# A gated cross-attention block: the next group's q, k and raw scores one body ahead, and norms from summed squares

## The chip, the cores and the metric

The kernel runs on one core of a Trainium2 chip. The metric is device time in microseconds (us). The kernel before takes 1311.98 us, the median of three runs (1311.91 to 1312.0). The engines are PE (TensorE), ACT (ScalarE), DVE (VectorE), POOL (GpSimd) and SP, which here only issues DMAs.

## The reference

The input x has 64 batches of 64 tokens with 256 features, and the context has the same shape. Four residual sub-blocks follow each other; the change touches the first.

```
def rms_norm(x, scale, eps=1e-6):
    ms = mean(square(x), axis=-1, keepdims=True)      # over all 16*128 = 2048 features
    return x * rsqrt(ms + eps) * scale
# 1. cross attention, 16 heads of 128
q   = rms_norm(layernorm(x) @ q_w + q_b, nq_s)        # split into heads after the norm
k   = rms_norm(ctx @ ki_w + ki_b, nki_s)
v   = ctx @ vi_w + vi_b
out = softmax(q k^T / sqrt(128)) v                    # in each batch and head, 64 x 64 scores
x   = x + tanh(g_xattn[0]) * (out @ o_w + o_b)
# 2. a dense layer plus the two best of 8 low-rank experts   3. a sigmoid attention on the raw context
# 4. the best of 8 larger experts; each with a layernorm before it and a tanh gate behind it
```

(The context is shorter than the reference's 257 image tokens, so the text branch is empty and only the image weights enter.)

## The kernel before

**Tiling.** The 4096 tokens are 8 groups of 512 (four tiles of 128 tokens, or 8 batches). Every engine runs its own program with the same skeleton: one body for each group b, and in it 16 steps, one for each head h. Products in float32 precision are made from a rounded high part and a remainder (`_hi`, `_lo`), three matmuls for each product (`three`, L113).

**One step** on PE is: scores of the last two heads (even steps only), `project` of k for head h (six matmuls of 512 columns), `attend` for head h-3, `values` for h, `project` of q for h, `prob_transpose` for h-2, `output` for h-3. The points "a" to "e" between them take side work (`share`): N is the next group's preparation (layernorm, transposes, norms), S the later sub-blocks of group b-1, T the last sub-block of group b-2. ACT copies every product out of its bank (`project`), takes the exponentials (`exps`) and rounds the attention output (`attn_hi`). DVE makes `logits`, `probabilities`, `attn_lo` and half of each copy `prob_copy`. Nothing but this written order and the semaphores sets the sequence. The products k, v, q use two banks in turn, and the scores of a pair of heads one bank, from which `logits` reads them directly.

**The norms.** The sum of squares of a token's 2048 q features is obtained without q: with the Gram matrix G = W W^T made once at the start (`turn_weight`, `gram_matrix`, 64 transposes and 128 matmuls), it is x G x^T plus terms in the bias. `gram_products` (L983) makes x G for each tile of x and context, `gram_sums` (L1503) multiplies with x and sums. `square_norms` and `norm_factors` take the reciprocal root on 8 columns, `norms` (L995) spreads the k factors over all rows with a matmul of ones and a diagonal, and `score_factors` (L1531) makes the 64 x 64 factors `rr` of each tile, by which `logits` multiplies.

**Weights.** The q and k weights stay in SBUF, as `w_hi` and `w_lo`. The v and output weights come from DRAM scratch in pairs of heads, 512 KB each, into two buffers.

```
        def step(b, h):                       # PE, L1255, cut
            if h % 2 == 0 and live(b, h - 2):
                scores(b, h - 2)
                scores(b, h - 1)
            project(b, h, 0)                  # k
            attend(b, h - ATT_LAG)            # ATT_LAG = 3
            values(b, h)
            project(b, h, 2)                  # q
            prob_transpose(b, h - TURN_LAG)   # TURN_LAG = 2
            output(b, h - OUT_LAG)            # OUT_LAG = 3
```

## Time and profile before

| | us |
|---|---|
| median of 3 runs | 1311.98 |
| the profiled execution | 1310.84 |
| its span | 1309.0 |
| PE busy | 1294.2 |
| DVE busy | 765.1 |
| ACT busy | 727.3 |
| POOL busy | 67.7 |

The span runs from the first to the last instruction of the profiled execution; 1.84 us of that run lie around it. The granted clock of TensorE was 1.00, which is 2.4 GHz, in all 40 slices of the span. Busy times are unions: matmuls are pipelined, so a matmul's printed duration is longer than the distance to the next one, and costs on PE are read as distances between starts.

### The profile page before, as it was taken

What the parts mean: (1) busy time and instruction counts of PE and PEld (TensorE: products, weight loads), DVE (VectorE), ACT (ScalarE), POOL (GpSimd) and SP (SyncE); (2) the same over time, 40 slices, a digit from 0 to 9 for tenths busy, and PEclk for the clock granted to TensorE, in tenths of its full rate; (3) what the DMA queues carried; (4) which work ended last, traced back from release to release, by engine and by line L of the source; (5) the groups of instructions that cost most, each with busy time, mean ns of one, the idle gap of its engine ahead of it and who ended that gap; (6) DMA issues with size and microseconds to landing.
All of it is one profiled execution on the core that took longest, in us unless ns stands there. A gap on an engine that the chain in (4) does not pass through costs nothing.

```text
span 1309.0 us, 26268 instructions
## 1 busy us (share of the span) xinstructions
PE 1294.2 (99%) x10249; PEld 1143.4 (87%) x10249; DVE 765.1 (58%) x2309; ACT 727.3 (56%) x2037; POOL 67.7 (5%) x112
## 2 busy tenths in 40 slices
PE   8999999999999999999999999999999999999998
PEld 8889889988998889988899888998889988898887
DVE  7645656646565565655556465564656646564585
ACT  4365756556465564655545655546646556556522
POOL 0000000000000000010000100001000000001010
PEclk9999999999999999999999999999999999999999
DMA  8221441132222231223212232123312112212101
GB/s 323 105 97 49 150 142 65 46 101 97 66 65 81 77 102 66 65 66 129 74 41 81 66 113 81 49 66 98 111 51 82 49 66 97 66 51 78 50 1 49
DMA packets 42985, 108.44 MB, mean 83 GB/s; under 512 B 3696, under 2 KB 22384, under 8 KB 42096
## 3 DMA queue, kind: packets, MB, share of 16 engines
q1 hardware_dynamic: 42864, 106.77, 24.1%
q8 instruction: 83, 1.36, 0.4%
q14 instruction: 38, 0.31, 0.1%
HBM read 94.17 MB, written 12.58 MB: 82 GB/s over the span
## 4 chain that ended last, share of the span: by engine, by line
PE 92%; DVE 4%; ACT 2%; issue 1%; DMA 1%; SPq 0%; DVEq 0%; ACTq 0%
PE bank L116 63%; PE bank L1022 8%; PE bank L1032 5%; PE bank L991 3%; PE bank L1132 2%; PE bank L1144 2%; PE bank L1011 2%; PE bank L1086 1%; PE bank L970 1%; PE bank L1176 1%; ACT logit L734 1%; DMA raw<-in_L_xattn_q_w_dram 1%; PE bank L998 0%; PE bank L1153 0%; DVE wt L1461 0%
## 5 line engine op out<-in xcount | busy, mean ns | idle before, releaser
L734 ACT ACTIVATE logit<-logit,least 128x64 f32<-128x64 f32 x512 | 171.1, 337 | 180.5 <-DVE least L1569 180.5
L116 PE MATMUL bank<-sv,ct_hi 128*128 128x256 f32 x1024 | 195.8, 290 | 0.0
L116 PE MATMUL bank<-so,ao_hi 128*128 128x256 f32 x1008 | 193.8, 291 | 0.1
L116 PEld LDWEIGHTS bank<-sv,ct_hi 128*128 128x128 f32 x1024 | 158.2, 188 | 13.1 <-issue 10.7
L116 PEld LDWEIGHTS bank<-so,ao_hi 128*128 128x128 f32 x1008 | 153.4, 188 | 7.8 <-issue 7.6
L1022 PEld LDWEIGHTS bank<-pt,v_sb 128*128 128x128 f32 x1024 | 133.7, 191 | 11.3 <-ACT pt L742 0.3
L116 PE MATMUL bank<-sv,ct_lo 128*128 128x256 f32 x512 | 142.8, 279 | 0.0
L752 ACT ACTIVATE v_sb<-bank 128x512 f32<-128x512 f32 x128 | 76.1, 594 | 119.6 <-PE bank L116 119.6
L116 PE MATMUL bank<-so,ao_lo 128*128 128x256 f32 x504 | 140.5, 279 | 0.0
L1557 DVE SCALAR_TENSOR_TENSOR ao_lo<-bank,vecs,ao_hi 128x512 fp32r<-128x512 f32 x126 | 94.6, 751 | 76.7 <-ACT ao_hi L728 76.5
L1022 PE MATMUL bank<-pt,v_sb 128*128 128x128 f32 x1024 | 134.8, 274 | 0.1
L755 ACT ACTIVATE q_sb<-bank,qbias,qscale 128x512 f32<-128x512 f32 x128 | 98.6, 770 | 50.6 <-PE bank L116 50.6
L1551 DVE COPY pt<-bank 64x256 f32<-64x256 f32 x128 | 54.8, 428 | 97.3 <-PE bank L1011 95.6
L116 PE MATMUL bank<-ct_hi,k_hi 128*128 128x512 f32 x256 | 109.1, 426 | 0.7 <-DVE ct_lo L1544 0.7
L116 PE MATMUL bank<-xt_hi,q_hi 128*128 128x512 f32 x256 | 104.2, 407 | 1.7 <-ACT k_sb L748 1.6
L748 ACT ACTIVATE k_sb<-bank,vecs 128x512 f32<-128x512 f32 x128 | 86.1, 673 | 29.4 <-PE bank L116 29.3
L116 PE MATMUL bank<-ct_lo,k_hi 128*128 128x512 f32 x256 | 101.1, 395 | 0.0
L116 PE MATMUL bank<-xt_lo,q_hi 128*128 128x512 f32 x256 | 101.1, 395 | 0.0
L116 PE MATMUL bank<-xt_hi,q_lo 128*128 128x512 f32 x256 | 101.0, 395 | 0.0
L116 PE MATMUL bank<-ct_hi,k_lo 128*128 128x512 f32 x256 | 101.0, 394 | 0.0
L734 ACT ACTIVATION_READ_ACCUMULATOR logit<-logit,least 128x1 f32 x512 | 97.0, 189 | 0.0
L116 PEld LDWEIGHTS bank<-sv,ct_lo 128*128 128x128 f32 x512 | 96.2, 188 | 0.0
(235 smaller groups left out, 2518.4 us busy)
## 6 DMA issues: line engine op xcount, KB each, us to landing
sv<-v_scratch SPq DMA_DIRECT2D x56, 512.0 KB, 3.4
so<-o_scratch SPq DMA_DIRECT2D x56, 512.0 KB, 3.3
xin<-in_x_dram SPq DMA_DIRECT2D x8, 512.0 KB, 4.5
cin<-in_ctx_pairs_dram SPq DMA_DIRECT2D x8, 512.0 KB, 5.8
cs<-in_ctx_turned_dram SPq DMA_DIRECT2D x8, 512.0 KB, 4.6
xres<-in_x_dram SPq DMA_DIRECT2D x8, 512.0 KB, 4.8
v_scratch<-sv SPq DMA_DIRECT2D x8, 512.0 KB, 2.8
o_scratch<-so SPq DMA_DIRECT2D x8, 512.0 KB, 2.8
```

The source lines that it names most:

```text
L116: last = pe.matmul(out, lhs[a], rhs[b], start=start and n == 0, stop=stop and n == 2, **kw)
L734: last = act.activation(logit[:, h % 2, t, :], logit[:, h % 2, t, :], ACT.Exp, scale=-1.0, bias=least[:, h % 2, t:t + 1], accum_out=rsum[: ...
L748: act.activation(k_sb[:, h % 2, :], bank[:, :], ACT.Identity, bias=vecs[:, 3 * H + h:3 * H + h + 1]).then_inc(pj_read.sem, 1)
L752: act.activation(v_sb[:, (h // 2) % 2, t:t + 2, :], bank[:, :].rearrange("p (t n) -> p t n", t=2), ACT.Copy).then_inc(pj_read.sem, 1)
L755: act.activation(q_sb[:, h % 2, :], bank[:, :], ACT.Identity, scale=qscale[:, h:h + 1], bias=qbias[:, h:h + 1]).then_inc(pj_read.sem, 1)
L991: last = pe.matmul(dst[:, c * P:D + 1], src[:, c, t * P:(t + 1) * P], gram[:, n, c, c * P:D + 1], start=c == 0, stop=c == DC - 1)
L1011: last = pe.transpose(bank[:, q * P:(q + 1) * P], prob[:, 2 * q:2 * q + 2, :].rearrange("p t l -> p (t l)"), ident[:, :])
L1022: last = pe.matmul(dst[:, q, i], v_sb[:, (h // 2) % 2, 2 * q + i, (h % 2) * HD:(h % 2 + 1) * HD], pt[:, q, i, :], start=True, stop=True)
L1032: last = pe.matmul(at_ps[i * SEQ:(i + 1) * SEQ, (h % 2 * NT + t) * SEQ:(h % 2 * NT + t + 1) * SEQ], q_sb[:, h % 2, s], k_sb[:, h % 2, keys ...
L1132: last = pe.matmul(dst[i][:, c * D:(c + 1) * D], xn[rows, t, c * P:(c + 1) * P], cin2[rows, t, :], start=True, stop=True)
L1551: dve.tensor_copy(pt_part(1), turned_probs(g, h, 1)).then_inc(pt_ready[1].sem, 1)
L1557: dve.scalar_tensor_tensor(out=lo[:, :], in0=attention_bank(g, h)[:, :], scalar=vecs[:, v:v + 1], in1=hi[:, :].bitcast(F32), op0=ALU.add, ...
```

## The change

There is one more body, b = -1. In body b the engines now make k, q and the scores of group b+1, while v, the softmax, the attention and the output are those of group b. The raw scores are copied by DVE into `raw_score` in SBUF (`score_copy`, one copy for two heads), and `logits` reads them there a body later. The last body makes no k, q or scores. Two context buffers alternate. The layernorm and transposes of a group come two bodies ahead.

The Gram matrices and products are gone. ACT squares q out of the bank (`project_q`); POOL squares k and adds both up over the heads (`add_squares`); in step 0 of group b's own body `norms` sums over partitions with a matmul of ones (k, as a row) and four one-column matmuls (q). DVE then takes the reciprocal root on 260 columns in step 1 (`score_factors`).

The q and k weights are split in body -1, written to DRAM scratch, and from group 1 on fetched in pairs of heads, 1 MB each, into two buffers (`fetch_weights`).

```diff
+        def add_squares(g, h):                                   # POOL, each head of each group
+            total = k_sum[:, g % 2, :], q_sum[:, g % 2, :]
+            pool.wait_ge(k_read.sem, k_read.count(g, h))
...
+            pool.tensor_tensor(k_sq[:, h % 2, :] if h else total[0], k_sb[:, h % 2, :], k_sb[:, h % 2, :],
+                               ALU.mult).then_inc(k_squared.sem, 1)
+            if h:
...
+                pool.tensor_tensor(total[0], total[0], k_sq[:, h % 2, :], ALU.add).then_inc(k_added.sem, 1)
+                pool.wait_ge(q_squared.sem, q_squared.count(g, h))
...
+                pool.tensor_tensor(total[1], total[1], q_sq[:, h % 2, :], ALU.add).then_inc(q_added.sem, 1)
...
+        def project_k(g, h):                                     # ACT
+            act.wait_ge(k_full.sem, k_full.count(g, h))
+            k_squared.wait(act, g, h - 2)
...
+        def project_q(g, h):                                     # ACT
+            act.wait_ge(q_full.sem, q_full.count(g, h))
...
+            if h:
+                q_added.wait(act, g, -1 if h == 1 else h - 3)
+            act.activation(q_sq[:, h % 2, :] if h else q_sum[:, g % 2, :], bank[:, :], ACT.Square,
+                           bias=vecs[:, h:h + 1]).then_inc(q_squared.sem, 1)
...
-        def gram_products(b, t):                                 # PE
...
-        def norms(b):
-            dst = take("rk", 0, b + 1)
-            pe.wait_ge(diag_ready.sem, diag_ready.count(b + 1, 0))
-            pe.matmul(dst[:, :], ones[:, :], diag[:, :, :].rearrange("p t n -> p (t n)"),
-                      start=True, stop=True).then_inc(rk_full.sem, 1)
+        def norms(g):
+            row, column = take("rk", 0, g), take("rq", 0, g)
+            pe.wait_ge(k_added.sem, k_added.count(g, H - 2))
+            pe.matmul(row[:, :], ones[:, :], k_sum[:, g % 2, :], start=True, stop=True)
+            pe.wait_ge(q_added.sem, q_added.count(g, H - 2))
+            for t in range(NT):
+                last = pe.matmul(column[:, t:t + 1], q_sum[:, g % 2, t * P:(t + 1) * P], ones[:, 0:1],
+                                 start=True, stop=True)
+            last.then_inc(rk_full.sem, 1)
...
         def step(b, h):                                          # PE
-            main = live(b, h)
...
+            main = live(b + 1, h)
+            if h % 2 == 0 and live(b + 1, h - 2):
+                scores(b + 1, h - 2)
+                scores(b + 1, h - 1)
+            if main and (b >= 0 or h >= FIRST_K):
+                project("k", b + 1, h)
             share(b, h, "a")
             if live(b, h - ATT_LAG):
                 attend(b, h - ATT_LAG)
             share(b, h, "b")
-            if main:
+            if live(b, h):
                 values(b, h)
             share(b, h, "c")
...
             if main:
+                project("q", b + 1, h)
...
-        def gram_sums(g, t):                                     # DVE
...
+        def score_factors(g):
...
+            rsqrt_guess(dve, chain, rqk[:, :], nqk_t[:, :], squares[:, :])
+            rsqrt_newton(dve, chain, rqk[:, :], nqk_t[:, :], squares[:, :], 3)
+            for t in range(NT):
+                last = dve.tensor_scalar(rr[:, g % 2, t, :], rqk[:, t * SEQ:(t + 1) * SEQ],
+                                         rqk[:, NT * SEQ + t:NT * SEQ + t + 1], -float(HD) ** -0.5, ALU.mult, ALU.mult)
             last.then_inc(rr_ready.sem, 1)
 
+        def score_copy(g, h):
+            dve.wait_ge(scores_full.sem, scores_full.count(g, h // 2))
+            at = h % H
+            dve.tensor_copy(raw_score[:, at:at + 2, :, :].rearrange("p h t l -> p (h t l)"),
+                            at_ps[:, :]).then_inc(scores_read.sem, 1)
...
-            chain.link(dve.tensor_tensor(logit[:, u, :, :], at_ps[:, u * NT * SEQ:(u + 1) * NT * SEQ].rearrange(
-                "p (t l) -> p t l", t=NT), rr[:, (g - (h < 0)) % 2, :, :], ALU.mult))
+            chain.link(dve.tensor_tensor(logit[:, u, :, :], raw_score[:, h % H, :, :], rr[:, (g - (h < 0)) % 2, :, :],
+                                         ALU.mult))
...
+            if "F" in parts:
+                if at == (0, "c"):
+                    mean_squares(b)
+                if at == (1, "b"):
+                    score_factors(b)
```

**PE at the start.** Before, in the order of the program (`raw` and `wt` are the q weights and their transpose); the same again for k follows the last row:

```order
L1294 MATMUL bank<-ident,ones 128x128 x3
L962 MATMUL bank<-ident,raw 128x128 x24
L970 MATMUL bank<-wt 128x257 x4
L970 MATMUL bank<-wt 128x129 x4
L962 MATMUL bank<-ident,raw 128x128 x4
L970 MATMUL bank<-wt 128x257 x4
```

Now (`wqk` is the buffer of q and k weights):

```order
L1349 MATMUL bank<-ident,ones 128x128 x24
L116 MATMUL bank<-ct_hi,wqk 128x512
L116 MATMUL bank<-ct_lo,wqk 128x512
L116 MATMUL bank<-ct_hi,wqk 128x512 x2
L116 MATMUL bank<-ct_lo,wqk 128x512
```

The first k product stands directly behind 24 matmuls that only keep PE at work; the transposes and Gram matrices are gone.

**POOL.** Before, all that it does up to the second group's work:

```order
L640 MEMSET pt 128x512
L646 TENSOR_TENSOR xres<-xres,obias 128x256 [waits xres_in,s_obias]
L646 TENSOR_TENSOR xres<-xres,obias 128x256 x3
L654 TENSOR_TENSOR xres<-xres,bias 128x256 [waits xn1_ready]
L654 TENSOR_TENSOR xres<-xres,bias 128x256 x3
```

Now, at the same place; the last three rows repeat for each head of each group:

```order
L696 MEMSET pt 128x512
L703 TENSOR_TENSOR k_sum<-k_sb 128x512 [waits k_read]
L703 TENSOR_TENSOR k_sq<-k_sb 128x512 [waits k_read]
L709 TENSOR_TENSOR k_sum<-k_sum,k_sq 128x512 [waits k_squared]
L713 TENSOR_TENSOR q_sum<-q_sum,q_sq 128x512 [waits q_squared]
L703 TENSOR_TENSOR k_sq<-k_sb 128x512 [waits k_read]
L709 TENSOR_TENSOR k_sum<-k_sum,k_sq 128x512 [waits k_added,k_squared]
L713 TENSOR_TENSOR q_sum<-q_sum,q_sq 128x512 [waits q_added,q_squared]
```

POOL has gained three operations of 512 columns for each head, and ACT waits for two of them.

**DVE in step 1 of a body** (here body 1; `pt` is the transposed probabilities, `squares` the mean squares). Before:

```order
L1557 SCALAR_TENSOR_TENSOR ao_lo<-bank5,vecs,ao_hi 128x512
L1551 COPY pt<-bank5 64x4x64
L1567 TENSOR_TENSOR logit<-bank4,rr 128x256
L1569 TENSOR_REDUCE least<-logit 128x4
L1567 TENSOR_TENSOR logit<-bank4,rr 128x256
```

Now; two more rounds of the last three rows and the four factors `rr` follow, and only then the copy `pt` and the logits:

```order
L1551 SCALAR_TENSOR_TENSOR ao_lo<-bank5,vecs,ao_hi 128x512
L74 TENSOR_SCALAR nqk_t<-squares 128x260
L75 TENSOR_SCALAR rqk<-nqk_t 128x260
L80 TENSOR_TENSOR nqk_t<-rqk 128x260
L81 SCALAR_TENSOR_TENSOR nqk_t<-nqk_t,squares 128x260
L82 SCALAR_TENSOR_TENSOR rqk<-nqk_t,rqk 128x260
```

A chain of eleven operations on 260 columns has moved in ahead of the copy that PE's `attend` waits for.

## Rows read from the trace of the kernel before

**Rows 1.** Busy time, share of the span and instructions of each engine.
```profile
PE 1294.2 (99%) x10249; PEld 1143.4 (87%) x10249; DVE 765.1 (58%) x2309; ACT 727.3 (56%) x2037; POOL 67.7 (5%) x112
```
**Rows 2.** Windows: stretch, length, busy us by engine, clock, DMA share, GB/s.
```profile
622.00:778.80 156.80, 156.69 (x1253) 138.60 (x1252) 90.97 (x282) 88.39 (x254) 8.32 (x12) 1.00 0.24 78
1091.00:1227.00 136.00, 135.90 (x1082) 119.39 (x1082) 73.36 (x208) 77.71 (x227) 8.32 (x12) 1.00 0.18 59
1238.00:1309.00 71.00, 63.48 (x453) 53.75 (x451) 48.70 (x151) 20.85 (x45) 5.11 (x8) 1.00 0.07 23
```
**Rows 3.** Timeline: start, us, engine, line, operation, count [idle before]; POOL.
```profile
682.02 3.01 POOL L654 TENSOR_TENSOR xres<-xres,bias 128x256 f32<-128x256 f32 x4 [95.79 <-ACT xn L761]
...
838.86 3.00 POOL L654 TENSOR_TENSOR xres<-xres,bias 128x256 f32<-128x256 f32 x4 [96.44 <-ACT xn L761]
```
**Rows 4.** Timeline of PE at the start and at one even step.
```profile
38.09 0.48 PE L116 MATMUL bank<-ct_hi,k_hi 128*128 128x512 f32 x1
...
39.57 0.82 PE L991 MATMUL bank<-gram,xs 128*128 128x257 f32 x4
...
44.74 0.48 PE L116 MATMUL bank<-sv,ct_hi 128*128 128x256 f32 x2
...
47.63 0.40 PE L116 MATMUL bank<-ct_hi,k_hi 128*128 128x512 f32 x1
...
49.03 0.40 PE L116 MATMUL bank<-sv,ct_hi 128*128 128x256 f32 x2
...
50.43 1.02 PE L998 MATMUL bank<-diag,ones 128*128 128x512 f32 x2
...
636.32 1.15 PE L1032 MATMUL bank<-k_sb,q_sb 128*64 128x64 f32 x32
```
**Rows 5.** Timeline of DVE and ACT at the start.
```profile
4.65 0.17 DVE L1902 TENSOR_TENSOR bsq<-vecs 128x16 f32<-128x16 f32 x1 [4.65 <-DMA vecs<-in_columns_dram]
...
11.40 1.40 DVE L1491 BATCH_NORM_STATS2 stats<-xin 128x6 f32<-128x256 f32 x4
...
14.92 0.37 DVE L87 BATCH_NORM_AGGREGATE moment<-stats 128x2 f32<-128x6 f32 x4
...
17.71 0.16 DVE L1500 SCALAR_TENSOR_TENSOR shift<-moment,rstd 128x4 f32<-128x4 f32 x1
...
17.91 2.08 ACT L708 ACTIVATE xin<-xin,shift,rstd 128x256 f32<-128x256 f32 x4
```
**Rows 6.** Groups by form on POOL: busy us, mean ns, idle before.
```profile
L654 POOL TENSOR_TENSOR xres<-xres,bias 128x256 f32<-128x256 f32 x32 | 23.8, 780 | 781.7 <-ACT xn L761 781.7
...
L664 POOL TENSOR_TENSOR x<-x,csum 128x256 f32<-128x256 f32 x24 | 15.0, 657 | 270.9 <-ACT xn L761 270.9
```
**Rows 7.** One line's durations: minimum/median/maximum ns.
```profile
L654 POOL TENSOR_TENSOR xres<-xres,bias x32: 724/737/938, 211.6 to 1256.2; 128x256 f32<-128x256 f32 x32
```
**Rows 8.** Groups by form on DVE and ACT.
```profile
L1461 DVE COPY wt<-bank 128x512 f32<-128x512 f32 x16 | 10.2, 685 | 3.9 <-PE bank L962 3.9
...
L1567 DVE TENSOR_TENSOR logit<-bank,rr 128x256 f32<-128x256 f32 x128 | 53.7, 420 | 56.2 <-PE bank L1032 54.8
...
L755 ACT ACTIVATE q_sb<-bank,qbias,qscale 128x512 f32<-128x512 f32 x128 | 98.6, 770 | 50.6 <-PE bank L116 50.6
```
**Rows 9.** Timeline of DVE in steps 0 to 2 and in step 6.
```profile
630.07 0.42 DVE L1576 TENSOR_TENSOR prob<-logit,rinv 128x256 f32<-128x256 f32 x1
...
634.47 0.43 DVE L1551 COPY pt<-bank 64x256 f32<-64x256 f32 x1 [2.48 <-PE bank L1011]
...
637.52 0.42 DVE L1567 TENSOR_TENSOR logit<-bank,rr 128x256 f32<-128x256 f32 x1 [1.02 <-PE bank L1032]
...
641.17 0.75 DVE L1557 SCALAR_TENSOR_TENSOR ao_lo<-bank,vecs,ao_hi 128x512 fp32r<-128x512 f32 x1 [0.63 <-ACT ao_hi L728]
...
683.51 0.92 DVE L1576 TENSOR_TENSOR prob<-logit,rinv 128x256 f32<-128x256 f32 x1
```
**Rows 10.** DMA issues: KB each, median us from issue to landing.
```profile
sv<-v_scratch SPq DMA_DIRECT2D x56, 512.0 KB, 3.4
```

More of the change, by code:

```diff
@@ L1051, in output, with bank_for @@
             last.then_inc(o_full.sem, 1)
-        def bank_for(g, u):
-            pj_read.wait(pe, g, u - 2)
-            return pj_ps[u % 2]
+        def bank_for(kind, g, h):
+            bank, before = PRODUCT[kind, g, h]
+            if before is not None:
+                kind_before, group, head = before
+                pe.wait_ge(READ[kind_before].sem, READ[kind_before].count(group, head))
+            return bank
         def values(g, h):
-            b, p = bank_for(g, 3 * h + 1), h // 2
+            b, p = bank_for("v", g, h), h // 2
+            ct_hi, ct_lo = context[g % 2]
             if is_body(g, 0):
@@ L1514, in square_norms @@
-        def square_norms(g):
-            dve.wait_ge(gr_read.sem, gr_read.count(g, 2 * NT - 1))
-            for n in range(2):
-                half = slice(n * NT, (n + 1) * NT)
-                chain.mark(dve.tensor_scalar(sums_b[:, half], sums[:, half], beta[:, n:n + 1],
-                                             1.0 / INNER, ALU.add, ALU.mult))
-            chain.wait()
-            chain.link(dve.tensor_scalar(sums_b[:, :], sums_b[:, :], RMS_EPS, None, ALU.add))
-            rsqrt_guess(dve, chain, rqk[:, :], nqk_t[:, :], sums_b[:, :])
-            rsqrt_newton(dve, chain, rqk[:, :], nqk_t[:, :], sums_b[:, :], 1)
@@ L1825, in step @@
                 logits(b, h - 1)
-            if main and h == 0 and not is_body(b, 0):
-                split(b, 1)
+            if h == 0 and 0 <= b < NG - 1:
+                split(b + 1, 1)
             if h % 2:
```

627 lines of the change are left out of this document (277 added, 350 removed).

## The prediction, made before the changed kernel ran

> **What bounds the kernel now.** I read the page's busy times first: PE is busy for 99% of the span, DVE for 58%, ACT for 56% and POOL for 5% [rows 1]. The windows say the same of one full body, PE 156.7 of 156.8 us [rows 2], and the bodies repeat at 838.86 - 682.02 = 156.8 us [rows 3]. TensorE's clock was granted at 1.00 (2.4 GHz) throughout. So before is a queue of PE work with hardly a gap: what leaves PE shortens the time one for one, as long as no other engine gets in its way. Only the tail from 1238 us on has waits, 7.5 us in 71 [rows 2], and the change leaves that alone. The questions are how much PE work goes, what the new first body costs, and whether DVE and POOL can still keep ahead.
>
> **PE work.** Costs are distances between starts. One k product is 49.03 - 47.63 = 1.40 us, one v product 50.43 - 49.03 = 1.40, the scores of two heads 1.15, the Gram products of one group 44.74 - 39.57 = 5.17 [rows 4]. The old `norms` matmul is at most its 1.02 us; I take 0.9. The new one adds four one-column products, which the trace does not show. From below a score matmul gives 1.15/32 = 0.036 us for each of eight passes, 0.3 us; from above, the old norms matmul once more, 0.9. I take 0.9, nearer to a full weight load, so new norms cost 1.8. A steady body then has 156.8 - 5.2 - 0.9 + 1.8 = 152.5 us of PE work.
>
> **The count.** I compare the two kernels at one point: in before, PE at 44.74 us, with k(0,0) and the Gram products of group 0 done; in after, PE as it leaves `norms` of group 0 in body 0. From 44.74 to the end of before are 1309.0 - 44.7 = 1264.3 us. Of these the new kernel has by then done, or never does:
> - 16 q and 16 more k products: 32 x 1.40 = 44.8
> - v(0,0): 1.4, and 16 heads of scores: 8 x 1.15 = 9.2
> - seven groups of Gram products: 7 x 5.17 = 36.2
> - eight old norms for seven new: 8 x 0.9 - 7 x 1.8 = -5.4
>
> Sum 86.2, so 1178.1 us of PE work remain behind that point.
>
> **When is that point?** The start: before, PE worked 38 us until the first k product [rows 4], on transposes and Gram matrices. These go, and what is late next is the input. Vectors landed at 4.65; the tokens, second in the old queue and now first, I put at 7. Behind them stand the statistics, 1.4, and variance and scale, 17.71 + 0.16 - 14.92 = 3.0, to 11.4. Then the normalising, 2.1 [rows 5], the rounding of q's first weights, the wait for k(0,1), the transposes' copies and the split of x; about 8.5 us by ACT and DVE operations of 0.6 to 1.2 each. So q(0,0) starts at 20 (17 to 25).
>
> In body -1 PE needs 2 x 1.40 + 0.58 = 3.4 us for each head. ACT needs less than 3. POOL does three operations of 512 columns. The trace has POOL only at 256 columns: 0.737 us with two full inputs, 0.612 to 0.657 where one is broadcast, 0.938 at worst [rows 6, 7]. Twice that bounds 512 columns between 1.22 (less if part is fixed cost) and 1.88; I take 1.4, just under twice 0.737, since both inputs are full. Three make 4.2, with the waits on itself 4.3 us a head. That is longer than PE's 3.4, and ACT waits for it: k of head h for the squares of h-2, q for the sum of h-3. So body -1 runs at POOL's pace. The first two heads' sums end at about 25; fourteen more take 60, to 85.4, and the norms end at 86.4. If PE set the pace it would be 75, with 1.88 us an operation 106.
>
> The Trainium skill ("GPSIMD Engine Reference", § 3.1) has 4497 ns for a POOL `tensor_tensor` add of 2048 columns; as an estimate that is 1.12 us for 512, 3.5 a head, and body -1 would be at PE's pace. This trace's 0.737 for 256 is above that rate, but part of it may be fixed. The sum would be 11 us less by the page.
>
> Without any new waits the span is 86.4 + 1178.1 = 1264.5 us.
>
> **DVE and POOL in the full bodies.** DVE had 91.0 us of work in 156.8 [rows 2]. It loses the Gram sums and gains eight copies of scores at 0.69 [rows 8] = 5.5, and eleven root steps on 260 columns at about 0.46 (0.42 for 256 columns [rows 8] and the link) = 5.1; net +3 us. The sum is hidden, but its place is not. In step 1 the chain and `rr`, some 6 us, stand ahead of the copy `pt`. Before, DVE sat idle for 2.48 us in front of that copy at 634.47, and 1.02 in front of the logits [rows 9]. So about 3.5 us are covered, `attend`, logits and `attn_lo` behind them are late by 2 to 3, and PE gets some of it. The logits no longer wait for scores, which gives part back. I take 1 us a body.
>
> POOL, idle before, is now at work for 16 x 4.3 + 8.3 = 77 us of a body. The trace shows what that does: `prob`, two SBUF inputs, takes 0.42 us, and 0.92 at 683.51, while POOL's bias additions run (682.02 to 685.03); one POOL operation in that line took 0.938 instead of 0.737 [rows 3, 7, 9]. Each waits for the other. The logits, which read a bank and `rr`, now read `raw_score` and `rr` and join this kind. With POOL at work half the time and 32 large and some 60 small such operations, I put +15 us on DVE: 109 of 152.5. That is covered on average, not where DVE was dense. I take 1 us a body of PE wait; nothing and 6 are the bounds. Together 2 x 7 = 14 us.
>
> This is the place of the Trainium skill's rule ("SBUF — State Buffer", § Who interferes with whom): a DVE instruction with two SBUF inputs contends with a GpSimd instruction that reads SBUF, and the loser blocks for the other's whole instruction. The row's 0.5 us against an operation of 0.74 agrees in kind. By full blocking the second rival below comes nearer.
>
> **The last body** has no k, q or scores: 136.0 - 44.8 - 8 = 83 us of PE. DVE keeps 73.4 - 1.2 = 72 [rows 2], 87%, in a chain exponentials - `prob` - transpose - `pt` - `attend` - `ao_hi` - `ao_lo` - `output` in which 2.8 us of cover a step are gone. I take 9 us of waiting, between 0 and 25.
>
> **ACT** gains one square a head (nearest row the q copy, 0.77 [rows 8]), 12 us on 88.4 of 152.5: hidden. **The weights:** 1 MB each two steps; 512 KB land in 3.4 us [rows 10], so about 7 against two steps of 9.5: hidden. In body -1 the writes of pair 2 queue behind 6 MB of loads and could hold ACT for a few us, where POOL is the bound anyway: nothing.
>
> **Sum.** 1264.5 + 14 + 9 = 1287.5 of span, +1.8 around it = 1289.3; the median shown stands 1.1 above the profiled run's 1310.84. Forecast **1290 us**.
>
> **Rivals.**
> 1. *Everything is covered.* POOL needs 3.6 us a head (-10), no waits in full bodies (-14), 4 in the last (-5): 1261 us. For it: in a full body PE waits for 0.1 us only [rows 2]. Against it: the row at 683.51 [rows 9].
> 2. *DVE becomes the bound in bodies 0 to 6 (slower).* The place is DVE beside POOL's 48 additions a body. DVE has 94 us of its own; if nearly each of POOL's 60 operations blocks it for 0.9 us or more, it reaches 94 + 54 = 148, and with its dependences PE waits for it. Each us over a body's 152.5 counts seven times; before's time is reached when a body waits 5.5 us rather than 2. At 8 us: 1290 + 7 x 6 = 1332. For it: the blocking is in the trace; against it: only half of each POOL operation blocked there.
> 3. *Body -1 is long.* POOL at 1.8 us an operation, or late weights: +15 to +20, 1308 us. For it: DVE's splitting of weights reads SBUF twice as well.
> 4. *The clock.* All rows show 1.00, the tail with 11% of waits too [rows 2]. In body -1 PE would be at work for 3.4 of 4.3 us. At 1.2 GHz a head takes 6.8, 16 x 2.5 = 40 us more: 1330. The Trainium skill ("TensorE: Matmul & The Clock Gate", Part 1) has the throttled state as the default that activity releases. No row here shows a fall.
>
> **Chances.** Forecast (1273 to 1305) 0.50; rival 1 0.20; rival 2 0.14; rival 3 0.12; rival 4 0.04. The range, from rival 1 to short of rival 2, is 1258 to 1325. A measurement tells 0.2%, 2.6 us, from no change. Slower takes most of rivals 2 and 4: 0.15; same 0.04; faster 0.81.
>
> **What would show it.** Right: the first k product at 13 us instead of 38; POOL without gaps in body -1 and `norms` of group 0 at about 86; bodies of 154 to 155 us by POOL's bias additions; `prob` and `logit` above 0.42 us in the mean; PE waits at `pt`, `attend` and `output` in step 2. Wrong: PE waits in every step (rival 2), a granted clock below 1.00 (4), or `norms` of group 0 before 78 or after 98 us.

## The result, and the profile after

The changed kernel takes 1423.8 us (median of 4 runs, 1418.5 to 1426.2) against 1312.0 (4 runs) for the kernel before on the same chip. The ratio is 1.085, 95% interval [1.083, 1.086]: slower by 112 us, where I had forecast 22 us faster. The range ended at 1325. The profiled execution took 1418.5 us, its span 1416.7; it is the fastest of the four, so differences of medians and of spans can disagree by some 5 us.

The page's busy line, as [rows 1]:

```profile
PE 1283.8 (91%) x9889; PEld 1114.4 (79%) x9889; DVE 878.7 (62%) x2164; ACT 802.1 (57%) x2177; POOL 522.2 (37%) x480
```

PE is busy for 10 us less than before, but the span is 108 us longer: PE waits for 133 us. DVE has 114 us more busy time. The windows, as [rows 2] (stretch, length, busy us of PE, PEld, DVE, ACT, POOL, clock, DMA share, GB/s): one full body, the last body, the tail.

```profile
611.73:782.56 170.83, 157.36 (x1228) 137.33 (x1228) 106.10 (x265) 97.31 (x269) 64.83 (x58) 0.98 0.35 118
1222.24:1345.70 123.46, 102.87 (x720) 91.23 (x720) 80.44 (x234) 63.14 (x219) 8.27 (x12) 0.93 0.22 73
1345.00:1416.70 71.70, 62.48 (x450) 53.28 (x448) 48.66 (x151) 20.41 (x43) 5.12 (x8) 1.00 0.07 23
```

The tail is what it was. A full body is 14 us longer, and PE is idle for 13.5 us of it. The periods come from POOL's bias additions, as in [rows 3]:

```profile
611.73 2.98 POOL L726 TENSOR_TENSOR xres<-xres,bias 128x256 f32<-128x256 f32 x4 [3.20 <-ACT xn L851]
...
782.56 2.98 POOL L726 TENSOR_TENSOR xres<-xres,bias 128x256 f32<-128x256 f32 x4 [3.20 <-ACT xn L851]
```

The start and both ends of the account, from PE's timeline (start, us, line, operands [idle before]): the first k product, q(0,0), and `norms` of groups 0 and 7, each with its one-column products (L1051) as its end.

```profile
12.62 0.76 PE L116 MATMUL bank<-ct_hi,wqk 128*128 128x512 f32 x1 [3.76 <-DVE wqk L1480]
...
22.45 0.77 PE L116 MATMUL bank<-xt_hi,wqk 128*128 128x512 f32 x1 [3.19 <-issue]
...
97.17 1.02 PE L1048 MATMUL bank<-k_sum,ones 128*128 128x512 f32 x2
98.12 1.05 PE L1051 MATMUL bank<-ones,q_sum 128*128 128x1 f32 x8
...
1222.24 1.10 PE L1048 MATMUL bank<-k_sum,ones 128*128 128x512 f32 x2 [0.94 <-issue]
1223.17 0.95 PE L1051 MATMUL bank<-ones,q_sum 128*128 128x1 f32 x8
```

Cut at the points where PE leaves `norms`, forecast and trace compare so:

```
                                  forecast   trace   difference
start to norms of group 0             86.4    99.2      +12.8
bodies 0 to 6                       1030.6  1124.9      +94.3
last body and tail                   170.5   192.6      +22.1
span                                1287.5  1416.7     +129.2
```

The forecast of the last row but one is the time of before behind v(7,0), from 1094.98 us, less 31 products of q and k and 16 heads of scores, plus 9 us of waiting: 1309.0 - 1095.0 - 43.4 - 9.2 + 9 = 170.5. It can't be taken from the recorded 83 us, since the window for it ended at 1227 [rows 2], and the last step of before's body was still to come:

```profile
1232.38 0.48 PE L116 MATMUL bank<-xt_hi,q_hi 128*128 128x512 f32 x1
```

**What a wait looks like.** Step 6 of a full body has PE's longest. DVE from 442.25 us, and POOL beside it:

```profile
442.25 0.88 DVE L1570 TENSOR_TENSOR prob<-logit,rinv 128x256 f32<-128x256 f32 x1
443.19 0.75 DVE L1551 SCALAR_TENSOR_TENSOR ao_lo<-bank,vecs,ao_hi 128x512 fp32r<-128x512 f32 x1
443.86 0.90 DVE L80 TENSOR_TENSOR nt_t<-rstd 128x4 f32<-128x4 f32 x1
444.79 0.16 DVE L81 SCALAR_TENSOR_TENSOR nt_t<-nt_t,var_eps 128x4 f32<-128x4 f32 x1
444.98 1.15 DVE L82 SCALAR_TENSOR_TENSOR rstd<-nt_t,rstd 128x4 f32<-128x4 f32 x1
446.17 0.16 DVE L80 TENSOR_TENSOR nt_t<-rstd 128x4 f32<-128x4 f32 x1
446.36 1.15 DVE L81 SCALAR_TENSOR_TENSOR nt_t<-nt_t,var_eps 128x4 f32<-128x4 f32 x1
...
449.01 0.68 DVE L1601 TENSOR_TENSOR x2t_lo<-bank,x2t_hi 128x512 fp32r<-128x512 f32 x1
```
```profile
443.70 1.04 POOL L703 TENSOR_TENSOR k_sq<-k_sb 128x512 f32<-128x512 f32 x1
444.81 1.30 POOL L709 TENSOR_TENSOR k_sum<-k_sum,k_sq 128x512 f32<-128x512 f32 x1
446.24 1.26 POOL L713 TENSOR_TENSOR q_sum<-q_sum,q_sq 128x512 f32<-128x512 f32 x1
```

Three operations on four columns, 0.16 us each by themselves, start while a POOL operation runs and end at most 0.02 us behind it: at 444.76, 446.13 and 447.51, where POOL ends at 444.74, 446.11 and 447.50. So DVE waits out the rest of POOL's instruction. Larger operations wait in the same way, but end later. In a `logit` of this kernel, POOL ends at 672.38, and DVE, which needs 0.42 by itself, at 672.66, 0.28 us behind:

```profile
671.09 1.29 POOL L713 TENSOR_TENSOR q_sum<-q_sum,q_sq 128x512 f32<-128x512 f32 x1 [0.94 <-ACT q_sq L845]
671.13 1.53 DVE L1561 TENSOR_TENSOR logit<-raw_score,rr 128x256 f32<-128x256 f32 x1
```

Back in step 6, `ao_lo`, with a bank and one SBUF tile as its two large inputs, takes its usual 0.75 [rows 9] in the same stretch. `x2t_lo` is late by 3 us, and PE waits:

```profile
449.84 0.66 PE L116 MATMUL bank<-late_w_hi,x2t_hi 128*128 128x392 f32 x1 [3.47 <-DVE x2t_lo L1601]
450.30 0.53 PE L116 MATMUL bank<-late_w_lo,x2t_hi 128*128 128x392 f32 x1
```
```profile
446.00:448.00 2.00, 0.37 (x4) 0.16 (x2) 1.83 (x6) 0.64 (x2) 1.37 (x2) 1.00 0.34 68
448.00:450.00 2.00, 0.16 (x1) 0.19 (x2) 1.90 (x6) 0.00 (x0) 0.00 (x0) 0.66 0.50 195
450.00:452.00 2.00, 2.00 (x7) 2.00 (x8) 1.97 (x3) 0.00 (x0) 0.00 (x0) 0.50 0.00 0
...
454.00:456.00 2.00, 2.00 (x11) 1.83 (x10) 0.19 (x2) 2.00 (x10) 0.00 (x0) 0.63 0.00 0
```

The granted clock (the number behind POOL's) falls from 1.00 to 0.50 (2.4 to 1.2 GHz) near the end of that idle stretch, and PE works on at half speed until about 455. Such a fall stands in each of bodies 0 to 5, and the last body, where PE waits most, has a mean of 0.93.

Over the run, the DVE forms with two SBUF inputs got longer, those with one did not (compare [rows 8, 9]):

```profile
L1561 DVE TENSOR_TENSOR logit<-raw_score,rr 128x256 f32<-128x256 f32 x128 | 76.0, 593 | 0.8
L1532 DVE COPY raw_score<-bank 128x512 f32<-128x512 f32 x64 | 43.6, 682 | 0.4
L82 DVE SCALAR_TENSOR_TENSOR rstd<-ntmp,rstd 128x4 f32<-128x4 f32 x72 | 24.6, 342 | 2.5
```

### The profile page after: what moved, and what is told of

It reads as the page before. It is cut to its first block, busy times and chain, and to the rows that moved or that the text cites. A ratio compares the mean times of both kernels' runs of the same rounds, so it can differ in the third digit from the quotient of the medians.

```text
span 1416.7 us, 26442 instructions
## 1 busy us (share of the span) xinstructions
PE 1283.8 (91%) x9889; PEld 1114.4 (79%) x9889; DVE 878.7 (62%) x2164; ACT 802.1 (57%) x2177; POOL 522.2 (37%) x480
## 3 DMA queue, kind: packets, MB, share of 16 engines
q8 instruction: 81, 1.33, 0.4%
## 4 chain that ended last, share of the span: by engine, by line
PE 54%; DVE 26%; ACT 12%; issue 5%; POOL 3%; DMA 0%; SPq 0%; POOLq 0%; ACTq 0%; DVEq 0%
PE bank L116 38%; PE bank L1076 5%; ACT logit L815 4%; ACT xn L851 2%; DVE rstd L82 2%; PE bank L1197 2%; PE bank L1209 2%; DVE ao_lo L1551 2%; PE bank L1087 2%; DVE stats L1586 2%; ACT k_sb L828 2%; PE bank L1065 1%; DVE ntmp L81 1%; ACT ao_hi L809 1%; POOL k_sum L709 1%
## 5 line engine op out<-in xcount | busy, mean ns | idle before, releaser
L703 POOL TENSOR_TENSOR k_sq<-k_sb 128x512 f32<-128x512 f32 x120 | 129.4, 1079 | 369.1 <-ACT k_sb L828 369.1
L713 POOL TENSOR_TENSOR q_sum<-q_sum,q_sq 128x512 f32<-128x512 f32 x120 | 160.0, 1333 | 263.3 <-ACT q_sq L845 262.5
L116 PE MATMUL bank<-xt_hi,wqk 128*128 128x512 f32 x512 | 190.2, 413 | 27.4 <-ACT k_sb L828 22.7
L116 PE MATMUL bank<-ct_hi,wqk 128*128 128x512 f32 x512 | 194.8, 422 | 10.1 <-ACT k_sb L828 4.5
L116 PE MATMUL bank<-so,ao_hi 128*128 128x256 f32 x1008 | 199.7, 296 | 1.5 <-DVE ao_lo L1551 1.3
L116 PEld LDWEIGHTS bank<-so,ao_hi 128*128 128x128 f32 x1008 | 158.4, 194 | 10.4 <-issue 10.0
L709 POOL TENSOR_TENSOR k_sum<-k_sum,k_sq 128x512 f32<-128x512 f32 x120 | 156.0, 1300 | 9.4
L116 PEld LDWEIGHTS bank<-xt_hi,wqk 128*128 128x128 f32 x512 | 98.8, 193 | 52.9 <-ACT k_sb L828 27.2
L116 PEld LDWEIGHTS bank<-ct_hi,wqk 128*128 128x128 f32 x512 | 100.3, 196 | 33.7 <-ACT k_sb L828 4.9
L1569 DVE RECIPROCAL rinv<-rsum 128x4 f32<-128x4 f32 x128 | 22.5, 176 | 143.7 <-ACT logit L815 143.5
L828 ACT ACTIVATE k_sb<-bank,vecs 128x512 f32<-128x512 f32 x128 | 86.4, 675 | 35.6 <-PE bank L116 35.4
```

The lines of the kernel that those rows point to most:

```text
L116: last = pe.matmul(out, lhs[a], rhs[b], start=start and n == 0, stop=stop and n == 2, **kw)
L703: pool.tensor_tensor(k_sq[:, h % 2, :] if h else total[0], k_sb[:, h % 2, :], k_sb[:, h % 2, :], ALU.mult).then_inc(k_squared.sem, 1)
L709: pool.tensor_tensor(total[0], total[0], k_sq[:, h % 2, :], ALU.add).then_inc(k_added.sem, 1)
L713: pool.tensor_tensor(total[1], total[1], q_sq[:, h % 2, :], ALU.add).then_inc(q_added.sem, 1)
L828: act.activation(k_sb[:, h % 2, :], PRODUCT["k", g, h][0][:, :], ACT.Identity, bias=vecs[:, 3 * H + h:3 * H + h + 1]).then_inc(k_read.sem, 1)
```

## The experiments

All were timed beside the kernel before, which stood at 1311 to 1312 us each time. "Body" is half the distance between two of POOL's bias additions that lie two full bodies apart; for the changed kernel it is 170.4 us.

**e1: POOL's additions on 8 columns.** The kernel leaves out the other columns' sums of squares of heads 1 to 15.
```diff
+            n = 8 if h else GT          # and [..., 0:n] in all three operations
-                pool.tensor_tensor(total[0], total[0], k_sq[:, h % 2, :], ALU.add)
+                pool.tensor_tensor(total[0][:, 0:n], total[0][:, 0:n], k_sq[:, h % 2, 0:n], ALU.add)
```


> POOL's square and its two additions of heads 1 to 15 work on 8 columns instead of 512 (this leaves the sums of squares of those heads out). Everything else, the order and every wait, stays. Theory 1, POOL blocks DVE: the changed kernel's full body takes 171 us for 152.5 us of PE work, and nearly all of the 18.5 go with POOL's traffic. Body 155 us, the whole 1418 - 5 x 15 - 2 x 8 = about 1325 us; the root chain of step 6 goes back from 1.15 to 0.16 us an operation and the clock stays at 1.00. Rival, DVE's new order: the copies of scores and the root chain stand in the way by themselves, POOL only colours their durations. Body 167 or more, the whole 1395 to 1418. The last body (POOL has nearly nothing to do there) stays at its 120 us by both.

Measured: 1338.2 us, ratio to before 1.020 [1.019, 1.022]. The window of one body, and two of the forms above:

```profile
573.33:731.23 157.90, 153.84 (x1229) 135.53 (x1228) 92.83 (x265) 97.58 (x269) 19.09 (x59) 1.00 0.38 127
```
```profile
L1562 DVE TENSOR_TENSOR logit<-raw_score,rr 128x256 f32<-128x256 f32 x128 | 54.4, 425 | 0.8
...
L82 DVE SCALAR_TENSOR_TENSOR rstd<-ntmp,rstd 128x4 f32<-128x4 f32 x72 | 11.7, 163 | 2.5
```

Theory 1 holds: with the same order and the same waits, 86 of the 112 us go, and the clock stays at 1.00 in the body. DVE's busy time falls by 13.3 us a body (106.1 to 92.8), close to my +15; the body shortens by 12.5. It was no wait for POOL's sums that went: in the changed kernel no wait of any engine between 224 and 1222 us ends with a result of POOL. The last body kept its length, as both theories said.

**e2: no root chain (the roots are left out). e3: tile_scales in step 4.**
```diff
-            rsqrt_guess(dve, chain, rqk[:, :], nqk_t[:, :], squares[:, :])
-            rsqrt_newton(dve, chain, rqk[:, :], nqk_t[:, :], squares[:, :], 3)
```


> The eleven operations of the root of the norms in step 1 are left out (the factors are made from the mean squares themselves, so the values are another); 5 us of DVE work in each of eight bodies. My forecast priced the place of this chain at 1 us a body: then 1410 us. Rival, the chain is bare wherever it stands: in the last body PE waited 2.99 + 1.94 us at attend and output just behind it, in a full body 0.91 + 1.82 at 565 to 570 us. Then 2.7 x 7 + 5 = 24 us go: 1395. If blocking stretches whatever DVE has (theory 1), less than that, since the work just slides: 1400 to 1410.

```diff
-                if at == (6, "a"):
+                if at == (4, "e"):
                     tile_scales()
```


> tile_scales, the ten small operations whose stretch to 4.5 us precedes PE's longest wait (3.5 us for x2t_lo in step 6), is moved from step 6 to the end of step 4; nothing is left out. If that wait and the half clock behind it are local, 3.5 + 4 us go in each of the bodies 1 to 6 that have it: 1418 - 5 x 7.5 = 1381 us and no clock below 1.00 in a full body. If DVE is late as a whole (theory 1 in its strong form), the wait comes back at the next dependence: under 10 us gained, 1408 or more.

Measured: e2 1390.7 us (1.060 [1.059, 1.062]), body 167.2; e3 1391.2 (1.061 [1.059, 1.062]), body 165.5. Five us of DVE in step 1 were worth 3.2 us a body and 3.6 in the last one with the tail, not my 1. Moving 4.5 us of DVE out of step 6, where nothing is left out, gave 5 of the 7.5 us a body that a local wait would.

**e4 and e5: matmuls without a use in the long wait.**
```diff
# e4: in front of mixture_rows(s, 0), behind its wait
+                        awake(take("xa", 0, s), 14)
# e5: in the bank of the next k product, ahead of the wait
+                if at == (6, "e") and b + 1 < NG:
+                    awake(bank_for("k", b + 1, 7), 14)
```


> Before PE's long wait in step 6, 14 matmuls of 512 columns without a use (14 x 0.23 = 3.2 us) fill it; nothing is left out. If the fall of the granted clock to 0.50 comes from the idle stretch, the clock stays at 1.00 there and half of the slow 8 us comes back: 4 us in each of five bodies, 1398 us. If the clock fell for another reason, the time stays or grows by up to 5 x 1 us.

> In e4 the matmuls without a use stood behind the wait, since their bank was the one that PE waited for. Here the same 14 (3.2 us) write the bank of the next k product and stand ahead of the wait in step 6; nothing is left out. If idleness of PE takes the clock down, the granted clock stays at 1.00 through step 6 and about 4 us come back in each of five or six bodies: 1418 - 22 = 1396 us. If the clock follows something else (POOL, DMA, the kind of work), it falls there all the same and the time is 1418 to 1424.

e4 missed its aim: 1443.0 us (1.100 [1.098, 1.102]). The bank itself is what PE waits for, so the filler ran behind the wait, its 14 matmuls in 6.05 us at a clock of 0.50 instead of 3.37 (e5), and made the profiled span 25 us longer. e5 stood right, and took 1416.7 (1.080 [1.079, 1.082]). Its step 6:

```profile
615.00:617.00 2.00, 2.00 (x14) 1.78 (x13) 1.93 (x3) 1.13 (x3) 1.87 (x2) 1.00 0.15 20
617.00:619.00 2.00, 2.00 (x10) 1.36 (x8) 1.83 (x8) 0.00 (x0) 0.02 (x1) 1.00 0.71 242
619.00:621.00 2.00, 1.68 (x10) 1.57 (x10) 1.94 (x4) 0.28 (x2) 0.00 (x0) 1.00 0.00 0
```

The clock stayed at 1.00 here: the idle stretch is what had taken it down. (It still fell three times elsewhere in bodies 1 to 6, where it falls five times in the changed kernel.) But the 22 us did not come: the profiled span is 1.6 us shorter and the median 7.1, so the falls in step 6 are worth some 2 to 7 us of the 112. That work done at half clock is made good at PE's next wait for DVE is my reading; no run shows it. The time does move with the clock from one execution to the next, 1418.5 us at a mean of 0.976 and 1426.2 at 0.970 in the changed kernel, 1315.5 at 0.995 and 1323.7 at 0.985 in e12; which of the two follows the other is open.

**e6: value and output weights asked for later.**
```diff
-        load_value_weights(0), load_value_weights(1), load_residual(0), oraw     # ahead of pair 2
+            if h in (5, 7):  load_value_weights(h // 2 - 2)                      # in the loop of body -1
+            if h == 9:       load_residual(0); oraw
```


> In SP's queue the value weights (2 MB), the residual's tokens and the output weights (2 MB) are asked for after pairs 4 and 5 of the q, k weights are on their way out, and no longer ahead of pair 2; nothing is left out. I had priced this queue at nothing. In the changed kernel ACT waited 5.85 us for the write of a pair, and PE 4.5 us behind it, at a clock of 0.66. If the queue is at fault: norms of group 0 at 91 instead of 97.2, the whole 1411. If POOL's pace is what holds body -1, as I forecast, no change: 1417 to 1419.

Measured: 1416.8 us (1.079 [1.078, 1.081]). The queue was at fault for one wait: in the changed kernel ACT waited with the rounding of pair 4 until pair 2 was written, and in e6 it doesn't (first fence after, second e6):

```profile
51.76 0.63 ACT L765 ACTIVATE wqk<-raw_k 128x512 fp32r<-128x512 f32 x1 [5.85 <-DMA qk_scratch<-wqk]
```
```profile
46.98 0.63 ACT L766 ACTIVATE wqk<-raw_k 128x512 fp32r<-128x512 f32 x1
```

`norms` of group 0 came 2.6 us sooner and the profiled span is 1.9 us shorter; the medians differ by 7, more than the spans can account for. While POOL works in body -1 most of the gain is taken back. e16 shows the rest.

**e8: logits at the end of the odd step. e9: e3, e6, e8 and the root chain in two pieces. e18: e9 without e8.**
```diff
-            if h % 2 == 0 and live(b, h - 2):      # start of the even step
-                logits(b, h - 2); logits(b, h - 1)
+            if h % 2 and live(b, h - 1):           # end of the odd step
+                logits(b, h - 1); logits(b, h)
```


> The logits of two heads, which DVE makes at the start of every even step, are made at the end of the odd step before it; all raw scores are there a body ahead, so nothing is left out. In the last body PE waits 1.8 to 2.9 us for prob in each even step, since logits, exponentials and prob follow each other there. If that dependence is the wait, the last body loses about 12 us and a full body 3 us: 1418 - 12 - 6 x 3 = 1388 us. If DVE's load as a whole (blocked by POOL, or 80 us of 123 in the last body) is the limit, the order doesn't matter: 1412 to 1424.

> The moves of e3, e6 and e8 together, and the root chain of the norms cut in two: two of its three Newton steps at the end of step 0, the third and rr after pt in step 1. Nothing is left out; POOL keeps its traffic. If the waits are separate places where DVE is late for a while, they add up: 1418 - 28 - 7 - 30 - 15 = 1338 us, still above before. If they share one cause that moves on to the next dependence (DVE slowed by POOL everywhere), 1365 to 1385.

> The changed kernel with e3's and e6's moves and the root chain of the norms cut in two as in e9, but with the logits where they were (e8 alone made it slower by 7 us). Nothing is left out. If e9's 1395 was held up by the early logits: 1418 - 27 - 5 - 10 = 1376 us. If each us of DVE's work is paid wherever it stands: 1388 to 1392.

Measured: e8 1425.5 us (1.086 [1.084, 1.089]), 1.7 above the changed kernel's median and so the same, not slower by 7, as the text of e18 has it by the profiled run of the changed kernel; its last body is longer by some 5 us; e9 1395.4 (1.064), body 167.2; e18 1392.2 (1.061), body 167.2. None adds to e3, which had as much alone. My reading that the even steps' waits in the last body come from the place of the logits fell with e8.

**e10 and e17: the old kernel with traffic of POOL alone, and with DVE work alone.**
```diff
# e10, POOL, each step
+                for n in range(4 * (16 * b + h), 4 * (16 * b + h) + 4):
+                    pool.wait_ge(s_extra, n)
+                    pool.tensor_tensor(extra, fixed[0], fixed[1], ALU.mult).then_inc(s_extra, 1)
# e17, DVE, each step, ahead of pt
+            for _ in range(2):
+                chain.link(dve.tensor_tensor(extra, fixed[0], fixed[1], ALU.mult))
```


> The kernel before, with POOL given work without a use: in each of 16 steps of each body four multiplications of 384 columns (1536 columns, as many as the changed kernel's three operations of 512), with two SBUF inputs that nobody writes. Nothing is left out. If POOL's reading alone slows DVE so that PE waits, the old order is hurt too: the changed kernel lost 13 us a body to it, so 8 x 13 = 105 us at most; the old order has 2.5 us of slack before pt and its logits read a bank, so I expect half, 1312 + 50 = 1360. If the blocking only hurts through the changed kernel's new DVE work, 1312 to 1320.

> The kernel before, with no POOL work added, and on DVE in each step, ahead of pt, two multiplications of 384 columns without a use: about 2 x 0.55 = 1.1 us, 17 us a body, close to what POOL's traffic put on DVE in e10 (91.1 to 105.8 us a body). Nothing is left out. If lateness of DVE is all that POOL's traffic does, whoever causes it, the time is like e10's: 1312 + 8 x 6 to 8 = 1360 to 1375. If POOL hurts in another way too (PE, ACT, memory), DVE's load alone is hidden in the old order with 91 of 157 us: 1312 to 1325.

Measured: e10 1374.2 us (1.047 [1.045, 1.050]), e17 1340.6 (1.022 [1.021, 1.024]). Two bodies of each:

```profile
546.83:876.21 329.38, 317.36 (x2503) 279.60 (x2502) 211.62 (x562) 177.17 (x505) 149.28 (x152) 0.99 0.22 74
```
```profile
539.20:859.12 319.92, 314.04 (x2503) 277.16 (x2502) 216.42 (x626) 177.11 (x505) 16.61 (x25) 1.00 0.23 77
```

So traffic of POOL by itself costs the old order 62 us, though that kernel has no other change. (POOL is busy for 75 us of a body there, 65 in the changed kernel.) Per body DVE gets 14.7 us more and the body 7.9. DVE work of its own, 17.1 us a body, costs 3.2. POOL's is the worse one, though it adds less. The operations that it stretches most are those of the root chains, which wait for one another (L81 of `ntmp` 312 ns in the mean instead of 162); that this is why it hurts more is my reading, no run separates it.

**e11: each POOL operation in four.**
```diff
+            for s in range(0, GT, GT // 4):
+                last = pool.tensor_tensor(out[:, s:s + GT // 4], a[:, s:s + GT // 4], b[:, s:s + GT // 4], op)
```


> Each POOL operation of 512 columns is cut into four of 128: the same columns, four times as many instructions; nothing is left out. If a DVE operation waits until POOL's whole instruction is done, the waits get shorter (up to 1.3 us before, then some 0.45 us, if 128 columns take that), while there are more of them: 1418 - 5 x 6 = about 1385. If POOL's fixed part makes it busy all the time (12 operations a head at 0.45 = 5.4 us), body -1 gets longer by 16 x 1.7 = 27 us and DVE is blocked as often: 1430 to 1450.

Measured: 1408.8 us (1.075 [1.072, 1.077]), body 167.2. POOL is busier (176.6 us in two bodies instead of 129.6), DVE less so (102.4 a body instead of 106.1). So shorter POOL instructions block for less, as the whole-instruction theory says, and body -1 pays: `norms` of group 0 starts at 108.1 instead of 97.2, and `bias` of body 1 stands at 276.9 instead of 270.8.

**e13 and e14: no additions on POOL, all on ACT and DVE.**
```diff
# ACT, in project_k
+            act.activation(k_sq[:, h % 2, :] if h else k_sum[:, g % 2, :], bank[:, :], ACT.Square, bias=...)
# DVE, each step ahead of share "b" (e13); in e14 in even steps behind share "e"
+                dve.tensor_tensor(total[:, g % 2, :], total[:, g % 2, :], new[:, h % 2, :], ALU.add)
```


> POOL adds nothing: ACT squares k as it does q (16 x 0.68 = 11 us more a body), and DVE makes the 32 additions of 512 columns (32 x 0.69 = 22 us more); with e3's and e6's moves. Nothing is left out. By theory 1 DVE then has 91 + 3 + 22 = 116 us of unblocked work instead of 106 of partly blocked: if blocking costs most by its length at the wrong places, the body is 160 to 163 us and the whole about 1355. If DVE's sheer load decides (more busy time than the changed kernel's 106), no better than e3 with e6: 1385 or more.

> As e13 (no POOL additions; ACT squares, DVE adds 22 us a body), but in even steps, where DVE also has logits, score copies and prob, the two additions stand behind pt and the residual work, at the step's end; in odd steps they stay ahead of pt. Nothing is left out. If the place decides, not the load: PE's waits in even steps go, body 171 to about 162, the whole 1423 - 5 x 9 - 10 = about 1370. If DVE's load decides, as e13 seems to say (109 us busy of 170, no better than blocked by POOL), the same within 5 us: 1418 to 1428.

Measured: e13 1423.0 us (1.084 [1.081, 1.086]), e14 1402.1 (1.069 [1.067, 1.071]). Their bodies:

```profile
612.22:783.28 171.06, 159.62 (x1229) 138.81 (x1228) 110.84 (x295) 105.82 (x285) 9.15 (x13) 0.97 0.35 117
```
```profile
599.68:767.39 167.71, 159.35 (x1228) 139.39 (x1227) 110.43 (x295) 105.94 (x285) 8.32 (x12) 0.97 0.35 120
```

With hardly any blocking left, work on DVE and ACT themselves makes the body as long as POOL did. Both runs hold e3's and e6's moves too, so their fair partner is e3 (body 165.5, 1391.2 us): against it e13 is 5 us a body and 32 in all slower. Moving half of DVE's additions behind `pt` gives 3 us a body back, not the 9 of "the place decides": both decide. What ACT's squares and its new waits for DVE's sums have in this, no run separates.

**e12 and e16: the change as if its new work were free** (sums and roots left out as in e1 and e2).
```diff
# e12 = e1 + e2 + e3; e16 = e12 + e6
```


> e1, e2 and e3 together: POOL's operations on 8 columns, no root chain, tile_scales in step 4 (leaves out the sums of squares of heads 1 to 15 and the roots). This is the changed kernel's PE order with a DVE that nobody blocks and that is 5 us shorter. If those two were all that stood between my 152.5 us of PE work and the 171 us, the body is 153 us and the whole 1338 - 6 x 5 - 5 = about 1303, and what is then left over my sum is the start and the last body. If the body stays above 156 us, a third cause (copies of scores, ACT) is in it: 1325 or more.

> e12 with e6's order of loads: no POOL traffic, no root chain, tile_scales early, loads late (leaves out the sums of squares of heads 1 to 15 and the roots). It asks what the change could be worth if its new work cost nothing. e12 was 1321 with PE's waits gone from the full bodies. If e6 takes the 4.5 us wait out of body -1 here, where POOL doesn't set the pace: 1321 - 7 = 1314, no faster than before. If the wait was only a cover for the next one, 1321.

Measured: e12 1321.0 us (1.007 [1.005, 1.008]), e16 1313.0 (1.000 [0.999, 1.001]).

```profile
566.07:721.72 155.65, 153.24 (x1229) 135.48 (x1228) 88.26 (x254) 97.91 (x269) 18.95 (x58) 1.00 0.38 130
```

PE works 153.2 us in a body of 155.7; my 152.5 was right to 0.5%. `norms` of group 0 stands at 93.1 us in e12 and at 84.5 in e16, so here e6 is worth 8 us in the median too. And still e16 only equals the kernel before.

**e15: PE work without a use in the last body.**
```diff
+            if b == LAST:
+                awake(bank_for("v", b, h), 6)          # where the k product was
+            if b == LAST and h + 1 < H:
+                awake(bank_for("v", b, h + 1), 6)      # where the q product was
```


> The changed kernel with 31 times six matmuls of 512 columns without a use (31 x 1.4 = 43 us of PE work) in the last body, where the old kernel had its k and q products; nothing is left out. The last body takes 120 us for 83 us of PE work by my sum. If the rest is a chain through DVE and ACT that PE's other work used to cover, most of the 43 us are free: 1418 + 10 = 1428, up to before's 136 us for the body. If the last body is bound by PE (I miscounted its work), the time grows by all of it: 1461.

Measured: 1437.4 us (1.096 [1.094, 1.098]), 13.6 more than without. The last body:

```profile
1225.59:1364.70 139.11, 135.57 (x900) 117.57 (x900) 81.02 (x234) 64.81 (x219) 8.47 (x12) 1.00 0.20 65
```

The last body grows from 123.5 to 139.1 us for 43 us of PE work; 27 of them are free. They come from two places: PE's waits shrink from 20.6 to 3.5 us, and with the clock at 1.00 instead of 0.93 PE's own work takes 92.6 us (135.6 - 43) instead of 102.9. So the last body is a chain through DVE and ACT which the k and q products had covered, and about 10 us of what looks like work there is work at half clock. How much of these 10 the chain would hide is not shown.

**One table over all.** A full body against DVE's busy time in it:

```
                              body    DVE    POOL
before                       156.8   91.1      8
e17 (old order, DVE work)    160.0  108.2      8
e10 (old order, POOL work)   164.7  105.8     75
e12, e16                     155.6   88.3     19
e1                           157.9   92.8     19
e2                           167.2  101.2     65
e11                          167.2  102.4     88
e3                           165.5  105.0     65
after                        170.4  106.1     65
e14                          167.8  110.4      8
e13                          170.4  111.0      9
```

In the new order, from e12 to e13, 22.8 us of DVE (and 8 of ACT, with other waits) cost 14.8 us of body. The first 4.6 cost 2.3, the 13 from e1 to after 12.5. In the old order there is more slack: 17 cost 3.2.

## Why the prediction was wrong

**The step that failed** is the one on DVE and POOL: "That is covered on average, not where DVE was dense. I take 1 us a body of PE wait; nothing and 6 are the bounds." The load was right: +15 us forecast, 13.3 measured between e1 and after. Turning it into waits was wrong by a factor of ten: 77 us in bodies 0 to 6 (`norms` of group 0 to `norms` of group 7 is 1125.1 us in after and 1048.5 in e1), 11 a body and outside my bounds. I had argued with the share, 109 of 152.5. But DVE, ACT and PE pass each head round in order (logits, exponentials, `prob`, transposes, `pt`, `attend`, `ao`), and an engine that is idle for 40% of the time is idle while it waits for the others: of DVE's idle time between 611 and 783 us, 18.7 us end with ACT's exponentials, 12.5 with PE's transposes and 9.4 with ACT's `ao_hi`.

**Within that step, the blocking** was read from one row: 0.92 us at 683.51, "only half of each POOL operation blocked there". That was a misreading. Of the four bias additions, which the row shows as one, the third stands so in before:

```profile
683.41 0.74 POOL L654 TENSOR_TENSOR xres<-xres,bias 128x256 f32<-128x256 f32 x1
```

`prob` started 0.10 us into it and ended at 684.43, 0.28 behind its end at 684.15, just as the logit above. So the blocking by the whole rest of an instruction stood in the row; that `prob` got longer by only 0.50 us hid it. The rows of after show the same for operations of 4 and of 256 columns. The Trainium skill ("SBUF — State Buffer", § Who interferes with whom) says that a DVE instruction with two SBUF inputs contends with a GpSimd one that reads SBUF, and one with a single SBUF input does not. The trace agrees: 1.15 us for an operation of 0.16, ended with POOL's, and 682 ns for the copy from a bank. I counted 32 large and some 60 small operations, but gave the small ones no weight where they stand in a chain; the operations of the root chains on four columns went from 0.16 us to between 0.20 and 0.42 in the mean, and one such chain made the 3.5 us wait.

**The root chain,** "1 us a body from its place": e2 gives 22 us in bodies 0 to 6, 3.2 each, with POOL at work. Without POOL's traffic it and `tile_scales` together are worth 2 (e1 against e12, 14 us in seven bodies). So 1 was about right for an unblocked DVE; the two terms don't simply add, each makes the other dearer.

**The last body,** "9 us of waiting, between 0 and 25": last body and tail took 22 us more than forecast, so the term should have been near 31: 20.6 us in which PE waits, and some 10 in which it works at half clock, which I had put at nothing. POOL is nearly idle there. Before hid the chain behind 43 us of q and k products that the change took away. I knew the chain, and priced it without going through it step by step. My 83 us of PE work for this body came from a window that leaves out its last step; 92.6 is what e15 shows. The sum of 1178.1 doesn't rest on the 83, but DVE's share of 87% does.

**The start.** "First k product at 13, q(0,0) at 20": 12.6 and 22.5. "Body -1 runs at POOL's pace": not shown, and at most a small part. POOL's operations took 1.04, 1.30 and 1.26 us where nothing stretched them (I took 1.4), and seven heads in a row without a gap, from 65.23 to 93.06 us, 4.0 us each instead of 4.3; PE was busy for 26.6 of the same 27.8 us. Before that POOL had gaps of 1.2 to 7 us, where I expected none, and PE waited for DVE and ACT in three places (2.8, 4.5 and 1.5 us), one of them behind the queue that I had priced at "nothing" (5.85 us for ACT). PE left `norms` at 99.2 instead of 86.4, past the 98 that I had named as a sign of being wrong. With POOL's work nearly gone (e1) `norms` starts only 3.7 us sooner, at 93.5; with the queue mended as well (e12 to e16) 8.6 more. The Trainium skill's rate ("GPSIMD Engine Reference", § 3.1), worked out to an estimate of 1.12 us, was nearer than mine for the square and below the additions.

**The PE work** was right to 1.2%: my 1178.1 us behind `norms` of group 0 hold 11.4 us in which before was idle, so 1166.7 of work; PE was busy for 1181.0 there in e12, part of it at a lower clock in the last body. The 0.9 us for the four one-column products, which no row showed, came out near: the trace has them as eight matmuls of 0.95 to 1.05 us together. Per body 152.5 against 153.2.

**The rivals.** Rival 2 (0.14) is what happened: it named DVE beside POOL and the point where it decides, 5.5 us a body. It expected PE to wait since DVE would fill the body, 148 of 152.5; DVE was at 106 of 170. It gave 1332, since it took 8 us of waiting a body; 17 were measured (170.4 for 153.2 of work), and the last body's 22 and the start's 13 came on top. Rival 4 (the clock) had no row and was 0.04: the clock did fall, in bodies 0 to 5 and in the last, behind PE's waits. In step 6 this cost 2 to 7 us (e5); what it cost in the last body no run separates.

**Could it have paid?** By the forecast PE's work was all that counted. e16 says no: with POOL's traffic, the roots' time and the queue's fault all taken away, the new order equals the old one. What a full body gains (1.2 us) and the shorter preparation give is taken by the last body's chain and by a body -1 of 85 us. No version here that computes everything came below 1391 us (e3), and none beats before. A cure for the last body was not tried.

## What to carry to other kernels

Busy shares don't say what an added microsecond costs. Where engines hand each head on in a loop, price it from the waits along the loop: in the new order here 13.3 us more on DVE cost 12.5, at 60% load, in the old one 17.1 cost 3.2. When work moves to GpSimd, list the DVE instructions with two SBUF inputs beside it, the tiny chained ones first: each can wait for nearly a whole GpSimd instruction. And when work is done a body ahead, look at the last body: the products that leave it were the cover for its chain.

## What the runs showed of the hardware

- A DVE operation with two SBUF inputs that starts while a POOL `tensor_tensor` runs waits for that instruction's end. With 4 columns it ends at most 0.02 us behind it (0.16 became 1.15 us), with 256 columns 0.28 us behind it (0.42 became 1.53 us). Copies from a bank (682 ns) and `ao_lo` with a bank and one SBUF tile (750 ns, at most 754, though 105 of the 126 started while POOL worked) kept their times.
- POOL operations of 128, 256 and 512 columns with f32 inputs took 0.41 to 0.51, 0.73 and 1.04 to 1.33 us, so by estimate a part of about 0.2 us is fixed; cutting them in four costs POOL 36% more time over two bodies (129.6 to 176.6 us) and still made the kernel faster by 15 us.
- TensorE's granted clock fell from 1.00 to 0.50 by the end of a wait of 3.5 us and stayed there for some 5 us in which PE always had work. With 3.4 us of matmuls without a use in the wait (e5) it stayed at 1.00, and the median fell by 7 us of 1424, the profiled span by 1.6.
